# Pairs of heads in pairs of banks: one exp and one maximum for two heads, the shift as a step of its own, and the row maxima standing late in each stretch

## What is computed

```python
q = jnp.einsum('ntc,hdc->nhtd', x_q, w_q)      # 16 heads of 64
k = jnp.einsum('ntc,hdc->nhtd', x_q, w_k)
v = jnp.einsum('ntc,hdc->nhtd', x_q, w_v)
a = jnp.einsum('nhtd,nhsd->nhts', q, k) / math.sqrt(q.shape[3])
a = jnp.where(causal_forbidden[None, None], -jnp.inf, a)
a = jax.nn.softmax(a, axis=3)
y = jnp.einsum('nhts,nhsd->nthd', a, v).reshape(a.shape[0], t, -1)
return y @ w_o
```

## Time and profile before

| | |
|---|---|
| median of 3 runs | 2251.08 us (2250.07 to 2251.12) |
| the profiled execution, its own time | 2248.06 us |
| its span in the profile | 2246.3 us |
| PE busy | 2132.8 us, 95% of the span |
| DVE busy | 1403.4 us, 62% |
| POOL busy | 1383.7 us, 62% |
| ACT busy | 939.8 us, 42% |
| granted PE clock, mean | 0.99 |

### The profile page before, as it was taken

One profiled execution on the slowest core, in us unless ns is written; L12 is line 12 of the kernel. 1 busy time (PEld: TensorE's weight loads), 2 busy tenths in 40 slices (PEclk: granted clock), 3 DMA queues, 4 the chain that ended last, 5 costly groups with the idle time before them and its releaser, 6 DMA issues.

```text
span 2246.3 us, 37109 instructions
## 1 busy us (share of the span) xinstructions
PE 2132.8 (95%) x13666; PEld 1604.2 (71%) x13666; DVE 1403.4 (62%) x3215; ACT 939.8 (42%) x1780; POOL 1383.7 (62%) x1242
## 2 busy tenths in 40 slices
PE   7998999999999999999999999899999899999998
PEld 5446888889766656766657666567666578889997
DVE  7375687776656566465764566765665736975654
ACT  6203543454344444244443344442444425434443
POOL 4313575777356676456674566664576756777774
PEclk9999999999999999999999999999999999999999
DMA  4524454555310001011001101100100135445552
GB/s 132 183 94 142 120 134 103 141 146 147 93 25 29 20 20 57 10 46 50 29 29 38 39 29 39 48 29 11 49 28 29 39 113 132 126 101 160 122 144 45
DMA packets 133796, 172.43 MB, mean 77 GB/s; under 512 B 16872, under 2 KB 109040, under 8 KB 133616
## 3 DMA queue, kind: packets, MB, share of 16 engines
q1 hardware_dynamic: 109040, 136.47, 18.7%
q0 software_dynamic: 24576, 33.57, 8.7%
HBM read 130.03 MB, written 39.85 MB: 76 GB/s over the span
## 4 chain that ended last, share of the span: by engine, by line
PE 72%; DVE 10%; issue 4%; POOL 3%; ACT 2%; DMA 1%; SPq 1%; another core or an unknown queue 0%; POOLq 0%; DVEq 0%; ACTq 0%
PE psum L1326 12%; PE psum L1477 11%; PE psum L1455 11%; PE psum L1347 11%; PE psum L1397 7%; PE psum L1502 4%; PE psum L1422 4%; PE psum L1411 4%; PE psum L1458 3%; PE psum L1487 3%; DVE f_hhi L2196 1%; DVE f_hlo L2198 1%; DVE t_neg L2257 1%; PE psum L1294 1%; DVE f_junk L2038 1%
## 5 line engine op out<-in xcount | busy, mean ns | idle before, releaser
L1761 ACT ACTIVATE t_p<-psum 128x512 f32<-128x512 f32 (+3 forms) x768 | 327.4, 492 | 328.5 <-PE psum L1458 316.6
L2458 POOL TENSOR_TENSOR t_acc<-t_acc,t_p 128x1024 f32<-128x1024 f32 (+3 forms) x256 | 421.4, 1646 | 32.1
L2377 POOL TENSOR_TENSOR f_wlo<-f_wst,f_whi 128x256 fp32r<-128x256 f32 x256 | 221.7, 926 | 153.5 <-ACT f_whi L1691 153.4
L1347 PE MATMUL psum<-f_whi,f_hhi 128*128 128x256 f32 x992 | 286.1, 288 | 6.9 <-DVE f_hlo L2198 6.9
L1347 PE MATMUL psum<-f_whi,f_hlo 128*128 128x256 f32 x992 | 280.3, 283 | 0.0
L1347 PE MATMUL psum<-f_wlo,f_hhi 128*128 128x256 f32 x992 | 280.2, 282 | 0.0
L2196 DVE CAST f_hhi<-f_h 128x512 fp32r<-128x512 f32 x256 | 142.7, 557 | 210.7 <-ACT f_h L1711 157.1
L2458 POOL TENSOR_TENSOR t_acc<-t_p 128x768 f32<-128x768 f32 x64 | 135.2, 2112 | 221.0 <-ACT t_p L1761 221.0
L1711 ACT ACTIVATE f_h<-psum 128x512 f32<-128x512 f32 x256 | 153.2, 599 | 277.2 <-PE psum L1326 243.1
L1477 PE MATMUL psum<-t_p,t_v 128*64 128x512 f32 (+3 forms) x1536 | 268.2, 491 | 0.2
L1477 PEld LDWEIGHTS psum<-t_p,t_v 128*64 128x64 f32 x1536 | 104.9, 137 | 160.7 <-issue 133.7
(11 more groups left out here) (301 smaller groups left out, 4608.4 us busy)
## 6 DMA issues: line engine op xcount, KB each, us to landing
f_wst<-in_L_ffn_w SPq DMA_DIRECT2D x64, 1024.0 KB
t_wk<-wkT SPq DMA_DIRECT2D x32, 256.0 KB, 2.6
t_wq<-wqT SPq DMA_DIRECT2D x32, 256.0 KB, 2.8
t_wv<-wvT SPq DMA_DIRECT2D x16, 512.0 KB, 3.7
normal<-f_xy SPq DMA_DIRECT2D x5, 1024.0 KB, 10.2
a_x<-in_L_attn_a_x SPq DMA_DIRECT2D x4, 1024.0 KB, 7.7
res<-a_x SPq DMA_DIRECT2D x32, 128.0 KB, 3.5
t_xy<-res SPq DMA_DIRECT2D x4, 1024.0 KB, 6.4
```

The costliest lines, as they stand in the source:

```text
L1347: m = pe.matmul(out, h[:, js], w[:, f, :], start=(f == 0 and a == 0 and j % 2 == 0), stop=(f == FT - 1 and a == 2), skip_group_check=True)
L1761: act.activation(p[:, i, q0:], k.bank[bank][:, q0:], ACT.Exp, scale=1.0 / float(np.sqrt(k.DH))).then_inc(k.drained[bank], 1)
L2377: m = pool.tensor_tensor(t["wlo"][n % 2][:, i, ks], t["wst"][:, i, ks], t["whi"][n % 2][:, i, ks].bitcast(F32), ALU.subtract)
L2458: pool.tensor_tensor(acc[:, :, q0:], (p0 if kt == 1 else acc)[:, :, q0:], p[:, :, q0:], ALU.add).then_inc(k.p_acc, 1)
```

## The change

1. **Pairs.** A score tile or a maximum tile takes two neighbouring banks (`work_pair`: 0 and 1, 2 and 3, or 4 and 5; a single bank left before a pair is skipped). Both heads count as one filling, and one instruction drains both: one exp over 2 x 512 elements, one plain reduction over 2 x 512. The masked reductions stay two.
2. **The shift is a step of its own** (`score_shift`), and the wait for `t_neg` goes with it. In the first stretch it stands behind M0 for S0; elsewhere right behind the tile's products.
3. **The order** in a stretch is S0 M0 S1 S2 M1 S3 M2 M3.
4. **DVE's order at a unit's end:** `t_neg` is made before `qk_low` of the first projection, not after it and the pumped steps. `divide(u, 0)` goes behind the last stretch (on PE, before its `weigh`), `normalize(u, 0)` to the end of `last_work`. The `rows` stream is no longer pumped after the middle stretch.
5. Output pieces go four at a time; some steps of `route` go together; and the maxima of unit 0, which run beside the experts, start an expert earlier, one tile a step.

```diff
         def row_halves(u, g):
             for i, (c, kt) in enumerate(k.stretch_tiles(g)):
                 self.scores(u, c, kt)
-                if u + 1 < U:
-                    self.row_max(u + 1, *maxima[g][i])
-                    self.part_max(u + 1, *maxima[g][i])
+                if i or g:
+                    self.score_shift(u, c, kt)
+                for part in maxima[g][(0, 1, 1, 2)[i]:(1, 1, 2, 4)[i]] if u + 1 < U else ():
+                    self.row_max(u + 1, *part)
+                    self.part_max(u + 1, *part)
+                if not (i or g):
+                    self.score_shift(u, c, kt)
                 yield
         def column_halves(u, g):
             if g == 0 and u:
                 self.divide(u - 1, 1)
+            elif g == 2 and u + 1 < U:
+                self.divide(u, 0)
...
-            if g == 1:
+            if g == 1 and u + 1 == U:
                 self.divide(u, 0)
                 normalize(u, 0)
...
         def last_work(u):
             if u + 2 < U:
-                yield from project(u + 2, 0)
+                self.qk_product(u + 2, 0)
             self.max_rows(u + 1)
+            if u + 2 < U:
+                self.qk_low(u + 2, 0)
+                yield
+                yield from project(u + 2, 2)
+            normalize(u, 0)
             yield
-            if u + 2 < U:
-                yield from project(u + 2, 2)
-            yield from pieces(3)
+            yield from pieces(KPC)
+            ready()
...
+    def work_pair(self):
+        while True:
+            i, ring = self.work % len(self.work_ring), self.work_ring
+            self.work += 1
+            if ring[i] % 2 == 0 and ring[i] + 1 in ring[i + 1:i + 2]:
+                self.work += 1
+                return ring[i]
...
-        for i in range(2):
-            bank = self.wait_filled(("st", u, c, kt, i))
-            act.activation(p[:, i, q0:], k.bank[bank][:, q0:], ACT.Exp,
-                           scale=1.0 / float(np.sqrt(k.DH))).then_inc(k.drained[bank], 1)
+        bank = self.wait_filled(("st", u, c, kt))
+        act.activation(p[:, :, q0:], k.pair(bank)[:, :, q0:], ACT.Exp,
+                       scale=1.0 / float(np.sqrt(k.DH))).then_inc(k.drained[bank], 1)
```

More of the change, by code:

```diff
@@ L966, in first_unit @@
             yield from project(0, 0, 2, 1, 3)
-            while self.turned < 2 * k.E - 1:
+            for part in sum(maxima, []):
+                self.row_max(0, *part)
+                self.part_max(0, *part)
                 yield
[L969 to L975, removed]
+                if self.turned == 2 * k.E - 1:
+                    self.work_ring = [6, 7, 0, 1]
             self.out_weights()
@@ L1049, in __init__, with wait_free @@
         self.uses = [0] * 8
+        self.last = {}
         self.work = 0
+    def wait_free(self, bank):
+        if bank in self.last:
+            by, n = self.last[bank]
+            self.wait_ge(self.k.drained[by], n)
     def take(self, key, bank, n=1):
-        k = self.k
-        if self.uses[bank]:
-            self.wait_ge(k.drained[bank], self.uses[bank])
+        for b in range(bank, bank + n):
+            self.wait_free(b)
         self.uses[bank] += 1
-        k.where[key] = bank, self.uses[bank]
+        for b in range(bank, bank + n):
+            self.last[b] = bank, self.uses[bank]
+        self.k.where[key] = bank, self.uses[bank]
         return bank
@@ L1418, in row_max @@
         self.wait_ge(k.a_qk, 2 * k.NC * u + (2 if n < k.KPC else 4))
-        banks = [self.take(("max", u, n, c, i), self.work_bank()) for i in range(2)]
-        for i, bank in enumerate(banks):
+        bank = self.take(("max", u, n, c), self.work_pair(), 2)
+        for i in range(2):
             hd = k.head_rows(i)
-            pe.matmul(k.bank[bank][:, 0:w], heads["qhi"][hd, n * P:(n + 1) * P], heads["khi"][hd, c * BANK:c * BANK + w],
-                      start=True, stop=True).then_inc(k.filled[bank], 1)
+            m = pe.matmul(k.bank[bank + i][:, 0:w], heads["qhi"][hd, n * P:(n + 1) * P],
+                          heads["khi"][hd, c * BANK:c * BANK + w], start=True, stop=True)
+        m.then_inc(k.filled[bank], 1)
     def max_rows(self, u):
@@ L1448, in scores, with score_shift @@
                 self.wait_drained(("qk", u, j))
[L1449 to L1451 removed]
+        bank = self.take(("st", u, c, kt), self.work_pair(), 2)
         for a, (keys, queries) in enumerate((("khi", "qhi"), ("khi", "qlo"), ("klo", "qhi"))):
[L1453 removed]
+            for i in range(2):
                 hd = k.head_rows(i)
[L1455 to L1456 removed]
+                pe.matmul(k.bank[bank + i][:, q0:], heads[keys][hd, ks], heads[queries][hd, qs], start=(a == 0),
+                          stop=False)
+    def score_shift(self, u, c, kt):
+        k, pe = self.k, self.e
+        q0, qs, _ = self.score_slices(c, kt)
+        bank, _ = k.where["st", u, c, kt]
+        neg = k.t["neg"][:].rearrange("p n j -> p (n j)")
+        self.wait_drained(("rows", u))
+        for i in range(2):
             hd = k.head_rows(i)
[L1458 to L1459 removed]
+            m = pe.matmul(k.bank[bank + i][:, q0:], k.ones[hd, :].bitcast(F32R), neg[hd, qs], start=False, stop=True)
+        m.then_inc(k.filled[bank], 1)
     def weigh(self, u, c, kt):
```

82 lines of the change are left out of this document (45 added, 37 removed).

## The result

The changed kernel takes 2321.1 us in the median of 4 runs (2319.2 to 2326.9), the kernel before 2251.1. The ratio is 1.032 (95% interval 1.030 to 1.034): **slower by 70 us**. The forecast had the sign and 43 of the 70 us. The profiled execution has a span of 2320.0 us and a mean granted clock of 0.981, against 2246.3 and 0.990. Two single executions in the later experiments, 5570 us in experiment 10 and 4140 us of the kernel before beside it, stand apart from all others and are left out of the times given.

A forecast was written before the change was run, and what follows sets the result against it. PE, busy 95% of the span, was taken to bound the kernel. Terms 16 + 19 + 14 + 1 - 1.75 - 4 - 1 = +43 us on the profiled 2248 gave 2291, as a median 2294 us; range 2262 to 2325.

The forecast's parts named there:

- the sign: Whole kernel: the change makes it slower, by +43 us; chance of slower 0.80.
- The ring of pairs: Attention stretches: eight pairs share three, so S2, M1, S3, M2 and M3 wait for earlier exps or maxima; +16 and +19 us.
- Middle stretches: Middle stretch of a unit, from S0 to `weigh`: 5.45 us against 4.94, +0.5 us, 31 times, +16.
- last ones: Last stretch of a unit: 4.8 us against 4.22, M3 behind M1's masked maximum; +0.6 us, 31 times, +19.
- The clean ends: Units' ends without `rows` or `route` steps stretching them: M0 replaces `t_neg` as PE's wait; +0.8 us 18 times, +0.05 12 times.
- I cost that at nothing: Loaded ends (`route` steps on DVE): steps delay M1 and M3 alike; nothing, bounds 0 to +1.5 us at about 8 ends.
- a rival with 1.5 us at 8 ends: Units' ends with `route` or `rows` steps: late DVE makes M0 hold PE, 1.5 us more at 8, 2306; chance 0.10.
- The start: End of unit 0's maxima, spread over a whole expert: the wait of 1.75 us goes, bounds 0 and twice that.
- The `rows` steps: Ahead of the last stretch: without pumped `rows` steps three waits of 1.3 us go; -4 us, bounds 0 and -4.
- Fewer fillings: PE counts 768 fewer fillings: nothing; as a rival, 0.01 us each, 8 us less, 2286, chance 0.05.

The follow-up runs named there:

- experiment 10: Changed kernel with single banks, `divide` and `normalize` behind the middle stretch, and unit 0's maxima as before the change; late maxima kept: 2214.6 us, ratio 0.986.
- experiment 3: Changed kernel with each head in a bank of its own again (two exps, two maxima, ring of seven): 2272.1 us, ratio 1.012.
- experiment 5: Changed kernel with single banks and `divide` and `normalize` of the first half back behind the middle stretch, late maxima kept: 2217.3 us, ratio 0.988.
- experiment 9: Kernel of experiment 5 with the ring cut from seven single banks to six: 2292.2 us, ratio 1.019.
- Experiment 2: Changed kernel with `divide` and `normalize` of the first half back behind the middle stretch, pairs and order kept: 2267.1 us, ratio 1.0095.
- experiment 8: The ladder: kernel of experiment 4 with 2 to 10 extra DVE reductions of 0.61 us ahead of `t_neg` at seven quiet ends: 2250.8 us, ratio 1.003.
- experiment 11: Kernel of experiment 10 with the `rows` stream pumped behind the middle stretch again: 2216.1 us, ratio 0.986.
- experiment 4: Changed kernel with single banks, the old order of maxima, and `divide` and `normalize` back behind the middle stretch: 2223.0 us, ratio 0.990.
- experiment 1: Changed kernel with the old order of maxima (S0 M0 S1 M1 S2 M2 S3 M3), all else kept: 2328.4 us, ratio 1.037.

## Why the prediction was right, and where it was short

- **The ring of pairs: right,** step by step. The joined exp of 512 columns took 1.025 us (1.02 taken), the joined maximum 1.223 (1.2). Middle stretches came out at +0.62 (+0.5 taken), since `weigh` starts 0.44 us behind M3 and not 0.34, last ones at +0.48 (+0.6): there M3 started 4.28 us behind S0 and not 4.4, still behind M1's maximum. That the two errors cancel is luck. Experiments 3, 5 and 9 show the cause to be the banks.
- **The clean ends: right.** `t_neg` was waited for no more and M0 took its place, +0.86 us (+0.8 taken) and +0.07 (+0.05). Experiment 2 shows the cause.
- **The step that failed is "I cost that at nothing"**, the loaded ends. I had the place and the steps of `route` on DVE, even a rival with 1.5 us at 8 ends; what I had not priced is what a long wait does to the engine behind it. In its place the runs show 22 us beyond the clean ends, 20 of them at loaded ends or beside them: longer waits (up to 3.29 us for `t_den`) and more low clock (17.1 us booked, 13.7 of it there). Two clean ends lost to the clock as well, 1.0 us each. Experiment 2 shows that `divide` and `normalize` at their new place bring the long waits, and experiment 8 that long waits bring the low clock. The trace of before held the hint, and I had read the mean clock of 0.99 and gone on: it has 10.2 us booked in this way at five places, four of them right behind the waits of S0 shown below. Had I counted the 8 loaded ends at 1.5 + 1.7 us each, the sum would have been 2320; that it comes so near owes something to luck, as the ends differ widely. The four waits, timeline of PE in the kernel before:

```profile
1103.02 0.50 PE L1455 MATMUL psum<-t_qhi,t_khi 64*128 64x512 f32 x2 [2.45 <-DVE t_neg L2257]
...
1373.09 0.50 PE L1455 MATMUL psum<-t_qhi,t_khi 64*128 64x512 f32 x2 [2.38 <-DVE t_neg L2257]
...
1479.50 0.49 PE L1455 MATMUL psum<-t_qhi,t_khi 64*128 64x512 f32 x2 [2.45 <-DVE t_neg L2257]
...
1612.56 0.51 PE L1455 MATMUL psum<-t_qhi,t_khi 64*128 64x512 f32 x2 [2.75 <-DVE t_neg L2257]
```

- **The start: wrong sign.** I counted the one wait that goes (1.75 us) and not the new ones that a ring of one pair brings; I had even written that small ones stand ahead of it. About +3 instead of -1.75.
- **The `rows` steps: right in place, nothing in total.** The -4 was seen in the three stretches and given back elsewhere (experiment 11).
- **Fewer fillings.** Nothing in these runs needs a price for them: pairs against six singles gained 20 us, and ACT's shorter drain covers what was seen of it (S2 starts at 2.37 us with pairs, 2.52 with six singles). A price for each filling by itself was neither shown nor isolated.

What stays open: how the 50 us of experiment 2 divide between clean ends, loaded ends and clock at each single end, and why the clock fell behind short waits: at two clean ends of the change, and at some ends of the ladder where nothing had been added.

## What to carry to other kernels

Before two buffers are joined into one, count the buffers in the ring as the joined form will see them: here an odd ring of seven became three, and the lost bank cost three times what the joined instructions saved. When a wait on the bound engine is removed, look at which instruction stands next in the queue and what its bank was last used for; a tile put forward as a filler must be the one that has nothing to wait for. A kernel at 95% of one engine can hold the gain and the loss in one change, so undo its parts one by one: what is left here is 1.4% faster than before.

## What the runs showed of the hardware

- A wait of PE can cost more than its length. With all waits of 2.2 to 3.3 us in the changed kernel, and of 2.5 to 4.9 in the ladder, the granted clock went to the lower level for a few microseconds, and the ladder's units paid 1.0 to 3.8 us on top of the wait; with the added waits of 1.3 and 1.9 it didn't. The length of one wait doesn't settle it: in the kernel before, the clock fell behind a wait of 2.38 us and not behind the one of 2.48; in the changed kernel it fell behind two of the waits of 1.2 us, and in experiment 4 behind waits of 1.0 and 0.8, while in experiment 1 it stayed up behind one of 3.16.
- PE counts as busy at the low clock: 4.74 of the 5 us at 1712 in the ladder, at a granted clock of 0.50. Its busy time rose by 41 us with the change and the same 13666 matmuls, but not by the clock alone: in experiment 9 it rose by 23 us with 1.7 us booked in the attention. The clock row and the distance of two starts tell.
- An exp over two banks takes 1.025 us against 2 x 0.596 by the mean, a plain maximum over two 1.223 against 2 x 0.684 in the ladder's kernel. But neighbours overlap: four single exps stand in 2.23 us, and single maxima start 0.61 us apart. By busy time, the exps of 192 full tiles fell from 208.2 to 196.3 us and the plain maxima from 152.4 to 149.0: joining saves ACT 0.06 us a tile and DVE next to nothing.
